# The last layer norm moved into the network's block, with its statistics taken in the attention's row additions

## The reference, cut to what matters

```
x = x + cross_attention(layer_norm(x, ln1...), ctx, wq1, ...)   # 16 heads of 128
x = x + cross_attention(layer_norm(x, ln2...), ctx, wq2, ...)
h = layer_norm(x, ln_mlp_scale, ln_mlp_offset)                  # mean and variance over 512 channels, eps 1e-5
h = gelu(h @ w_fc1 + b_fc1) @ w_fc2 + b_fc2                     # 512 -> 2048 -> 512
return x + h
```

## Time and profile before

| what | us |
|---|---|
| median of 3 runs | 2793.92 (2788.14 to 2794.48) |
| profiled execution, its own time | 2796.03 |
| its span | 2794.3 |
| PE / DVE / ACT / POOL busy | 2504.8 / 1397.7 / 1140.4 / 1112.1 |
| mean granted TensorE clock | 0.941 |

### The profile page before, as it was taken

How to read it: one execution, slowest core, us unless ns; L and a number is a source line. 1 busy time by engine, 2 the same in 40 slices (tenths; PEclk the granted TensorE clock), 3 DMA queues, 4 the chain that set the end, 5 groups by cost and what they waited for, 6 DMA issues and landing times. The chain is left out here.

```text
span 2794.3 us, 37817 instructions
## 1 busy us (share of the span) xinstructions
PE 2504.8 (90%) x14008; PEld 2190.1 (78%) x14008; DVE 1397.7 (50%) x2347; ACT 1140.4 (41%) x2439; POOL 1112.1 (40%) x494
## 2 busy tenths in 40 slices
PE   7888489779998788899979999998998999999698
PEld 5665334468895555689969999988997899999698
DVE  4666621278885531223345566643334466665643
ACT  3776111222323211122356566641235566665321
POOL 1100322141111110162168879755323878877300
PEclk9999669989998889999989999998998999999899
DMA  7552601489992014062854445425275544442300
GB/s 228 120 124 70 221 24 40 143 213 239 239 226 92 1 61 149 22 209 101 276 169 155 144 153 167 146 62 175 114 240 184 163 152 135 154 150 93 117 31 24
DMA packets 215850, 385.68 MB, mean 138 GB/s; under 512 B 88740, under 2 KB 127676, under 8 KB 215028
## 3 DMA queue, kind: packets, MB, share of 16 engines
q1 hardware_dynamic: 215668, 383.28, 44.3%
HBM read 288.03 MB, written 103.35 MB: 140 GB/s over the span
## 5 line engine op out<-in xcount | busy, mean ns | idle before, releaser
L1732 PE MATMUL att_ring<-ca_pp,att_arena 128*128 128x400 f32 (+1 forms) x2304 | 438.5, 349 | 27.0 <-POOL att_arena L1814 16.8
L1732 PEld LDWEIGHTS att_ring<-ca_pp,att_arena 128*128 128x128 f32 (+1 forms) x2304 | 423.0, 191 | 36.5 <-POOL att_arena L1814 22.5
L1803 POOL TENSOR_TENSOR att_arena<-att_arena 128x1448 fp32r<-128x1448 f32 x64 | 212.1, 3313 | 254.6 <-ACT att_arena L1820 254.6
L1732 PE MATMUL att_ring<-att_arena,qk_wh 128*128 128x362 f32 x1024 | 256.8, 332 | 0.0
L2416 DVE TENSOR_TENSOR ca_yl<-att_ring,att_arena 128x400 fp32r<-128x400 f32 x256 | 146.7, 573 | 204.8 <-ACT att_arena L2375 204.8
L1814 POOL TENSOR_TENSOR att_arena<-state_X,att_arena 128x1536 fp32r<-128x1536 f32 x64 | 224.3, 3505 | 5.0
L1732 PE MATMUL rec_fbank<-rec_fch,rec_fwl 128*128 128x362 f32 x512 | 174.9, 342 | 24.9 <-POOL rec_fwl L1031 16.0
L1811 POOL TENSOR_TENSOR att_arena<-state_X,att_nothing 128x1536 fp32r<-128x1536 f32 x64 | 175.9, 2749 | 49.5 <-DMA state_X<-in_ctx 49.5
L1732 PE MATMUL att_ring<-att_arena,qk_wl 128*128 128x362 f32 x512 | 173.4, 339 | 18.5 <-POOL att_arena L1997 18.1
L1732 PEld LDWEIGHTS att_ring<-att_arena,qk_wh 128*128 128x128 f32 x1024 | 186.0, 193 | 0.0
L1732 PE MATMUL rec_fbank<-rec_fcl,rec_fwh 128*128 128x362 f32 x512 | 170.7, 333 | 0.0
(11 more groups left out here) (379 smaller groups left out, 5874.0 us busy)
## 6 DMA issues: line engine op xcount, KB each, us to landing
att_arena<-keys SPq DMA_DIRECT2D x64, 724.0 KB, 5.3
state_X<-in_ctx SPq DMA_DIRECT2D x64, 512.0 KB, 3.9
rec_vb<-kept_value SPq DMA_DIRECT2D x256, 100.0 KB, 5.3
queries<-att_arena SPq DMA_DIRECT2D x16, 1600.0 KB
att_arena<-queries SPq DMA_DIRECT2D x64, 400.0 KB
keys<-rec_stage SPq DMA_DIRECT2D x32, 724.0 KB, 4.2
keys<-att_kstage SPq DMA_DIRECT2D x32, 724.0 KB, 3.3
state_X<-in_ctx SPq DMA_DIRECT2D x64, 210.0 KB, 4.1
```

The source lines that it names most:

```text
L1732: issued = nc.tensor.matmul(out, x, y, start=(first and k == 0), stop=(last and k == count - 1))
L1803: self.nc.gpsimd.tensor_tensor(self.kl[:, n % 2].bitcast(F32R), self.kl[:, n % 2], self.kh[:, n % 2].bitcast(F32), ALU.subtract).then_inc( ...
```

## The change

- `attention` gets a tile `stats`. In `add_rows` VectorE waits for its own addition and takes the batch's bn_stats into it. `stats` is allocated in `program` and passed in both calls of `attention_block`; `mlp` reads it.
- `mlp` has a single block. The separate blocks for the statistics and for the norm are gone; their instructions stand in the lists of the network's block. Normalised rows and affine values lie in a part of `mixedT`, the transposed ones in the four `outs` banks.
- The loads are issued by SP in the block: first matrix in two pieces with a semaphore each, small tensors, second matrix.
- The norm's first four batches come ahead of the tiles, with piece 0 of the first matrix rounded after batch 0 (ScalarE) and subtracted after batch 1's affine (VectorE). TensorE transposes batches 0 to 4 and begins the tiles when four batches have their low part.
- In the first four tiles: after Gelu 0 piece 1 is rounded and subtracted; after tile n's Gelu and subtraction VectorE normalises batch 5 + n and applies the affine to batch 4 + n; TensorE transposes batch 4 + n ahead of tile n's products, for n = 1, 2, 3.
- The second matrix is split after u = 4 instead of u = 1. GpSimd adds the bias rows after Gelu 15.

The diff, without signatures, semaphore declarations and comments:

```diff
...
                 nc.vector.tensor_tensor(X[:, b, :], X[:, b, :], bank_of("rows", half, i)[0:L, :], ALU.add).then_inc(rows_added, 1)
+                dve.wait_ge(rows_added, b + 1)
+                nc.vector.bn_stats(stats[:, b, :], X[:, b, :])
...
-        start_copies(nc, raw_in[0], loads(0)[0:1])
-        start_copies(nc, raw_in[1], loads(0)[1:2])
-        start_copies(nc, small_in, [(bias[:], a["fc1_columns"]), (row[:], a["fc2_rows"])])
-        layer_norm_transposed(nc, "lnm", X, 1e-5, column("L3_xattn_ln_mlp_scale"), column("L3_xattn_ln_mlp_offset"),
-                              ident, lambda b: (highT[:, b], lowT[:, b]), "split")
+        first_raw_in = [sc.sem(f"first_raw_in{i}") for i in range(2)]
...
+        room = mixedT[:].rearrange("p c n -> p (c n)")
+        xn = room[0:L, 0:2 * C].rearrange("l (i c) -> l i c", i=2)
+        affine = room[:, 2 * C:2 * C + 2 * CC * L].rearrange("p (i c l) -> p i c l", i=2, c=CC)
+        turned = [[outs[2 * i + part][:].rearrange("p (c l) -> p c l", c=CC) for part in range(2)] for i in range(2)]
+        moments = sc.sb("moments", [L, B, 2])
...
+            for dst, src, arrived in zip(pieces(raw[0][:], 0), (fc1[:, :, i * FP * P:(i + 1) * FP * P] for i in range(PIECES)), first_raw_in):
+                sp.dma_start(dst, src).then_inc(arrived, 16)
+            sp.dma_start(bias[:], a["fc1_columns"]).then_inc(small_in, 16)
+            sp.dma_start(row[:], a["fc2_rows"]).then_inc(small_in, 16)
+            sp.dma_start(*loads(0)[1]).then_inc(raw_in[1], 16)
...
         def _(pool):
+            for b in range(B):
+                pool.wait_ge(norm_high, b + 1)
+                nc.gpsimd.tensor_tensor(lowT[:, b], affine[:, b % 2], highT[:, b].bitcast(F32), ALU.subtract).then_inc(norm_low, 1)
             pool.wait_ge(small_in, 32)
+            pool.wait_ge(xn_ready, B)
+            pool.wait_ge(gelu_done, HIDDEN)
             for b in range(B):
-
                 nc.gpsimd.tensor_tensor(X[:, b, :], X[:, b, :], row[:], ALU.add).then_inc(row_added, 1)
         @block.scalar
         def _(act):
+            def first_high(i):
+                act.wait_ge(first_raw_in[i], 16)
+                nc.scalar.activation(pieces(wh[0][:], 0)[i], pieces(raw[0][:], 0)[i], ACT.Copy).then_inc(high_w, 1)
+
+            def normal_high(b):
+                act.wait_ge(turned_ready, b + 1)
+                if b >= 2:
+                    act.wait_ge(norm_low, b - 1)
+                for c in range(CD, CC):
+                    nc.scalar.activation(affine[:, b % 2, c, :], turned[b % 2][1][:, c, 0:L], ACT.Identity, bias=offset[:, c:c + 1],
+                                         scale=scale[:, c:c + 1]).then_inc(affine_act, 1)
+                act.wait_ge(affine_dve, CD * (b + 1))
+                act.wait_ge(affine_act, CD * (b + 1))
+                nc.scalar.activation(highT[:, b], affine[:, b % 2], ACT.Copy).then_inc(norm_high, 1)
+
             def high(part, m):
-                act.wait_ge(raw_in[m], 16 * part + 16)
+                act.wait_ge(raw_in[m], 16 * part + 16 * m)
                 if part:
                     act.wait_ge((full, out_full)[m], (HIDDEN, OUTS)[m] * part)
                 for dst, src in zip(pieces(wh[m][:], m), pieces(raw[m][:], m)):
                     nc.scalar.activation(dst, src, ACT.Copy).then_inc(high_w, 1)
+            act.wait_ge(var_ready, 1)
+            nc.scalar.activation(std[:], vareps[:], ACT.Sqrt).then_inc(std_ready, 1)
+            for b in range(BH):
+                normal_high(b)
+                if b == 0:
+                    first_high(0)
             act.wait_ge(small_in, 32)
-            high(0, 0)
             for part in range(PARTS):
                 for u in range(HIDDEN):
                     n = HIDDEN * part + u
@@ -2613,24 +2651,60 @@
                     f = FT * part + u % FT
                     nc.scalar.activation(act32[:, u % 2, :], ring[u % RING][:, 0:HALF], ACT.Gelu,
                                          bias=bias[:, f:f + 1]).then_inc(gelu_done, 1)
-                    if u == 1:
+                    if n == 0:
+                        first_high(1)
+                    if n < BH:
+                        normal_high(BH + n)
+                    if u == BH:
                         high(part, 1)
...
+            def low_piece(part, m, i):
+                dve.wait_ge(high_w, PIECES * (2 * part + m) + i + 1)
+                nc.vector.tensor_tensor(pieces(wl[m][:], m)[i], pieces(raw[m][:], m)[i], pieces(wh[m][:], m)[i].bitcast(F32),
+                                        ALU.subtract).then_inc(weight_ready, 1)
+
             def low(part, m):
-                for i, (dst, src, rounded) in enumerate(zip(pieces(wl[m][:], m), pieces(raw[m][:], m), pieces(wh[m][:], m))):
-                    dve.wait_ge(high_w, PIECES * (2 * part + m) + i + 1)
-                    nc.vector.tensor_tensor(dst, src, rounded.bitcast(F32), ALU.subtract).then_inc(weight_ready, 1)
+                for i in range(PIECES):
+                    low_piece(part, m, i)
+
+            def normalise(b):
+                if b >= 2:
+                    dve.wait_ge(turned_ready, b - 1)
+                nc.vector.tensor_scalar(xn[:, b % 2, :], X[:, b, :], mean[:, b:b + 1], rstd[:, b:b + 1],
+                                        ALU.subtract, ALU.mult).then_inc(xn_ready, 1)
+
+            def affine_low(b):
+                dve.wait_ge(turned_ready, b + 1)
+                if b >= 2:
+                    dve.wait_ge(norm_low, b - 1)
+                for c in range(CD):
+                    nc.vector.tensor_scalar(affine[:, b % 2, c, :], turned[b % 2][0][:, c, 0:L], scale[:, c:c + 1], offset[:, c:c + 1],
+                                            ALU.mult, ALU.add).then_inc(affine_dve, 1)
...
-            low(0, 0)
+            for b in range(B):
+                nc.vector.bn_aggr(moments[:, b, :], stats[:, b, :]).then_inc(moments_done, 1)
+            dve.wait_ge(moments_done, B)
+            nc.vector.tensor_scalar(vareps[:], moments[:, :, 1], 1e-5, None, ALU.add).then_inc(var_ready, 1)
+            nc.vector.tensor_copy(mean[:], moments[:, :, 0]).then_inc(mean_done, 1)
+            dve.wait_ge(std_ready, 1)
+            nc.vector.reciprocal(rstd[:], std[:]).then_inc(rstd_ready, 1)
+            dve.wait_ge(rstd_ready, 1)
+            dve.wait_ge(mean_done, 1)
+            normalise(0)
+            for b in range(BH):
+                normalise(b + 1)
+                affine_low(b)
+                if b == 1:
+                    low_piece(0, 0, 0)
             for part in range(PARTS):
...
-                    if u == 1:
+                    if n == 0:
+                        low_piece(0, 0, 1)
+                    if n < BH:
+                        if BH + n + 1 < B:
+                            normalise(BH + n + 1)
+                        affine_low(BH + n)
+                    if u == BH:
                         low(part, 1)
...
+            def transposes(b):
+                pe.wait_ge(xn_ready, b + 1)
+                if b >= 2:
+                    pe.wait_ge(affine_dve, CD * (b - 1))
+                    pe.wait_ge(affine_act, CD * (b - 1))
+                for c in range(CC):
+                    last = nc.tensor.transpose(turned[b % 2][c // CD][:, c, 0:L], xn[:, b % 2, c * P:(c + 1) * P], ident[0:L, 0:L])
+                last.then_inc(turned_ready, 1)
+
+            for b in range(BH + 1):
+                transposes(b)
             for part in range(PARTS):
                 for half in range(2):
+                    if part == 0:
+                        pe.wait_ge(norm_low, BH * (half + 1))
                     for f in range(FT):
                         n = HIDDEN * part + FT * half + f
+                        if 1 <= n < BH:
+                            transposes(BH + n)
                         pe.wait_ge(weight_ready, PIECES * 2 * part + f // FP + 1)
...
-        attention(nc, f"ca{i}", t, X, weights, scratch)
+        attention(nc, f"ca{i}", t, X, weights, scratch, stats)
...
+        stats = sc.sb("stats", [L, B, 6])
...
```

More of the change, by code:

```diff
@@ L2221, in _, with attention @@
                     t.scores(pe, 1)
-def attention(nc, prefix, t, X, weights, scratch):
+def attention(nc, prefix, t, X, weights, scratch, stats):
     HALVES = STEPS // BH
@@ L2526, in _, with mlp @@
             turn_rows(1)
-def mlp(nc, a, X, ident, column, out, output_gone):
+def mlp(nc, a, X, ident, column, out, output_gone, stats):
     FH = F3 // 2
@@ L2533, in mlp @@
     PARTS = 2
+    CD = CC // 2
+    scale, offset = column("L3_xattn_ln_mlp_scale"), column("L3_xattn_ln_mlp_offset")
     with Scope(nc, "mlp") as sc:
@@ L2560, in mlp @@
         mixedT = sc.sb("mixedT", [P, CC, B * L])
+        room = mixedT[:].rearrange("p c n -> p (c n)")
[3 more added lines that the diff above has]
+        moments = sc.sb("moments", [L, B, 2])
+        mean, vareps, std, rstd = (sc.sb(n, [L, B]) for n in ("mean", "vareps", "std", "rstd"))
```

(11 more changed lines are left out.)

## The result

| | kernel before | changed kernel |
|---|---|---|
| median of 4 runs each | 2793.72 us (2788.14 to 2794.48) | 2819.93 us (2810.16 to 2824.36) |
| ratio, 95% interval | | 1.0088 [1.0067, 1.0108] |
| profiled execution (span) | 2796.03 (2794.3) | 2810.16 (2808.4) |

The change made the kernel slower, as forecast, but by 26.2 us of medians where the steps came to 16.5. The profiled execution of the changed kernel is the fastest of its four; it had run 4.9 us ahead of the kernel before when it came to the first place that the change touches.

A forecast was written before the change was run, and what follows sets the result against it. The last stage was taken as bound by a prologue on other engines, then TensorE's nearly gapless stream. 5.8 - 4.9 + 11.6 + 4.0 = +16.5 us took the median from 2793.92 to 2810.4 us, range 2800 to 2818.

The forecast's parts named there:

- A: Statistics in the row additions, first attention: addition and statistics pairs 1.33 us apart, without cover, cost +5.8 us.
- B: From the last attention's additions to the first product: first product at 2636.4 against 2641.27, -4.9 us.
- C: Stream's first tiles: TensorE's transposes wait behind the previous tile's Gelu; +6.1 us, then +2.8 us twice, together +11.6 us.
- D: TensorE's clock after the waits before tiles 1 to 3: partly half speed, +4.0 us (0 to 6.6).
- The Gelu's table load: Before tile 0's Gelu: the load fits into ScalarE's idle time after its last rounding, with no cost of its own.
- 1: Rival on the stream's clock: same waits but clock kept, D = 0; +12.5 us, 2806.4; chance 0.22.
- 3: Rival on the first tiles: normalisations 5, 6, 7 done in time, so not slower; +2.3 us, 2796.2; chance 0.12.
- 4: Rival: as 3, and the statistics find cover in the row additions; -9.3 us, 2784.6; chance 0.04.
- 2: Rival: all three tiles at the low clock and the first weight piece late; +22.3 us, 2816.2; chance 0.12.

The follow-up runs named there:

- e1_again: The changed kernel run anew with no edit: 2813.01 us, ratio 1.0093 to the kernel before.
- e4: The kernel before with only an unused tile of 192 bytes a partition allocated ahead of all layers: 2798.54 us, ratio 1.0030.
- e16: The kernel before with an unused tile of 448 bytes a partition at the same place: ratio 1.0031, plus 8.7 us.
- e14: The changed kernel with its statistics tile padded from 192 to 256 bytes a partition: 2809.28 us, ratio 1.0059.
- e3: The changed kernel with 48 extra, overwritten products put into TensorE's waits ahead of the transposes of batches 5, 6 and 7: ratio 1.0074.
- e5: The changed kernel with normalisations one batch ahead and transposes of batches 5, 6, 7 ahead of tiles 1, 3, 5: 2803.6 us, ratio 1.0056.
- e11: The changed kernel with statistics in the network's block, no shared tile, earlier first-piece rounding and Gelu table, spread transposes: 2787.87 us, 0.9986 of the kernel before.
- e15: As e11, but with batch 7's transposes moved from tile 5 to tile 4: 2786.81 us, 0.9979 of the kernel before.

## Why the prediction was right and where it failed

- **Direction and order of the parts**: right. Slower, and the stream's waits are the largest part.
- **A**: +5.8 forecast, +6.05 and +6.2 in the traces. Pairs 1.33 us apart; the next block's load follows the last of them, as before. The mechanism was right.
- **B**: from the row additions to the first product 26.4 us forecast, 2638.38 - 2612.11 = 26.3 measured. The weight piece landed in 5.1 us, and the boundary took 1.58.
- **C**: waits of 5.6, 2.3 and 2.3 us forecast. Measured 6.61, of which 1.3 is the table load, and 2.15 twice. Half 0's eight tiles took 36.6 us, 34.4 forecast. Spreading the transposes took C and D away together.
- **A step that failed, small**: "The Gelu's table load fits between ScalarE's last rounding and tile 0's end". There was room, 5.22 us of it, and the load did not use it: it ran when the Gelu's product was there, 1.3 us. In the timeline of the kernel before it ran ahead of the stream's first product (2641.27), and only the Gelu waited:

```profile
2640.35 1.28 ACT L2614 ACT_TABLE_LOAD   x1
```

- **D**: +4.0 forecast, 4.7 in the first trace of the changed kernel and 6.0 in that of e1_again, so this term was low. Taking half of 1.7 us for each of the two shorter waits was too little: behind each of them the granted clock was at its lower level, 0.50 from 2655.4 to 2658.8 and 0.51 from 2662.2 to 2665.7, with TensorE busy in all of it.

```profile
2655.40:2658.80 3.40, 3.40 (x13) 3.37 (x14) 0.41 (x2) 0.54 (x1) 1.04 (x1) 0.50 0.03 13
2662.20:2665.70 3.50, 3.50 (x13) 3.48 (x12) 0.12 (x1) 0.54 (x1) 1.05 (x1) 0.51 0.00 0
```

By the rule that the prediction cited from the Trainium skill ("TensorE: Matmul & The Clock Gate", section "HAM oscillation — how this bites in real kernels") D would have been 6.6, an estimate; the two traces lie below it, the second one near it.
- **The step that failed in size is the sum itself**: "5.8 - 4.9 + 11.6 + 4.0 = +16.5 us" has no term for the tile that all layers now lie behind. I read the allocation in the diff and priced it at nothing without a word. It costs 8 us (e4, e16) in a kernel whose code is the same, and with its shift padded away the changed kernel stands at +16.5 (e14). With the tile's 8.4 us the sum is +24.9, and with 1.3 for the table load +26.2; the ratios say +24.6 and +25.9. The range ended at 2818, below the measured 2819.93, because its unknowns were all local.
- **Rivals**: 1 (clock kept) falls by e3 and the granted clocks; 3 and 4 by TensorE's three waits; 4 also by additions 1.33 us apart; 2 came nearest (2816.2 for 2819.93), but by half for a wrong reason: the clock did cost more than forecast, while the first piece was not late (5.1 us).

## What to carry to other kernels

An in-order queue that takes a transpose into a stream inherits the whole chain behind that transpose: put it as many tiles later as its operand's chain is long, and most of the cost goes (e5: 13 to 15 us of the traced stretch). Look also at what a helper adds for its other callers, and at what an allocation moves: a new tile ahead of everything is better padded to a multiple of 256 bytes, which here gave 9 us back (e14), or kept in the scope that uses it, as in e11 and e15, and a price for it belongs in the sum. When every traced step fits and the total does not, test the parts of the diff that hold no instruction.

## What the hardware showed unexpectedly

- Unused SBUF bytes per partition ahead of all tiles: 192 cost 8.4 us and 448 8.7, 256 cost 0.8 (not to be told from nothing), of 2790. GpSimd's 128x1536 subtraction took 3541 to 3550 ns (medians of the ten profiles with such a shift) instead of 3508 to 3510 (the seven others).
- A VectorE operation of 100x4 lasted 9.17 us, until three consecutive GpSimd operations had ended; its shortest is 0.16 us.
- ScalarE's table load for a Gelu (1.28 us) ran before its operand's wait in one kernel and behind it in the other, with idle time ahead of it in both. The runs don't show what decides this.
